# Attention with a sparse feed-forward: the third value product behind the next step's first maxima, the turn of the maxima behind the third maxima

## The reference, cut to what matters

```python
h = layernorm(x)                                  # x: 16 x 512 x 128
q, k, v = (h @ w_lat @ w_heads for each)          # 16 heads of 8
att = softmax(where(causal, q k^T / sqrt(8), -inf))
x = x + layernorm(att v @ w_proj + b_proj)
y = shared_geglu(layernorm(x)) + sum over the top 2 of 12 experts of w_e * geglu_e(layernorm(x))
x = x + layernorm(y)
```

## Time and profile before

| what | value |
|---|---|
| runs | 1266.59, 1270.77, 1272.27 us; median 1270.77 |
| the profiled execution | 1269.61 us, span 1267.8 us |
| mean granted TensorE clock | 0.930 |
| PE busy | 1074.8 us, 85% of the span |
| DVE busy | 837.0 us, 66% |
| ACT busy | 745.3 us, 59% |
| POOL busy | 631.4 us, 50% |

### The profile page before, as it was taken

One profiled execution on the slowest core, in us unless ns is written; L12 is line 12 of the kernel. 1 busy time (PEld: TensorE's weight loads), 2 busy tenths in 40 slices (PEclk: granted clock), 3 DMA queues, 4 the chain that ended last, 5 costly groups with the idle time before them and its releaser, 6 DMA issues.

```text
span 1267.8 us, 31490 instructions
## 1 busy us (share of the span) xinstructions
PE 1074.8 (85%) x8446; PEld 619.5 (49%) x8446; DVE 837.0 (66%) x2411; ACT 745.3 (59%) x1311; POOL 631.4 (50%) x1184
## 2 busy tenths in 40 slices
PE   4789999999999999978888877655899999999765
PEld 2633333333333333323565545322788888888732
DVE  7587777777878777766875556322466666666637
ACT  3777777777767777756544344321566666666616
POOL 4256666666666666644145545554144444444344
PEclk9799999999999999989767887778899999999988
DMA  8223333333333333332611111111222222221156
GB/s 221 69 74 88 96 101 101 91 90 97 95 94 93 96 101 99 91 104 62 223 31 39 37 37 35 37 37 56 51 67 61 62 66 60 62 67 51 47 192 215
DMA packets 135607, 107.47 MB, mean 85 GB/s; under 512 B 32204, under 2 KB 127875, under 8 KB 135539
## 3 DMA queue, kind: packets, MB, share of 16 engines
q1 hardware_dynamic: 124722, 87.45, 24.6%
q0 software_dynamic: 8544, 17.78, 3.9%
q10 hardware_dynamic: 2272, 1.45, 0.4%
HBM read 55.96 MB, written 50.69 MB: 84 GB/s over the span
## 4 chain that ended last, share of the span: by engine, by line
PE 62%; DVE 10%; issue 9%; another core or an unknown queue 7%; ACT 7%; DMA 3%; SPq 1%; ACTq 1%; POOL 0%; DVEq 0%; POOLq 0%
PE ps L1221 11%; PE ps L1386 7%; PE ps L1387 7%; PE ps L1398 7%; DVE maxima L1524 5%; PE ps L1149 5%; PE ps L1180 5%; PE ps L1140 2%; PE ps L1313 2%; PE ps L1332 2%; PE ps L1157 2%; ACT quad_area L973 2%; PE ps L1203 1%; ACT outT_area L918 1%
## 5 line engine op out<-in xcount | busy, mean ns | idle before, releaser
L1524 DVE TENSOR_REDUCE maxima<-ps 128x8 f32<-128x1024 f32 x320 | 387.0, 1222 | 122.6 <-PE ps L1149 109.3
L911 ACT ACTIVATE pT_area<-ps 128x1024 f32<-128x1024 f32 x320 | 327.5, 1025 | 145.1 <-PE ps L1180 144.5
L699 POOL TENSOR_SCALAR_AFFINE_SELECT pT_area<-pT_area 128x256 f32<-128x256 f32 (+1 forms) x448 | 190.4, 439 | 110.9 <-ACT pT_area L911 109.1
L801 POOL DMA_INDIRECT ys_dram<-quad_area,place_cur x139 | 133.1, 957 | 206.3 <-issue 138.2
L791 POOL DMA_INDIRECT xs_dram<-quad_area,idx_cur x128 | 123.3, 963 | 139.5 <-issue 73.0
L1221 PE MATMUL ps<-pT_area,quad_area 128*32 128x512 f32 (+3 forms) x2048 | 190.9, 446 | 0.0
L1180 PE MATMUL ps<-quad_area 64*128 64x512 bf16 (+3 forms) x1024 | 124.9, 301 | 25.5 <-DVE maxima L1524 22.2
L1386 PE MATMUL ps<-quad_area 128*128 128x256 f32 (+1 forms) x456 | 129.8, 367 | 8.1 <-issue 6.8
L1387 PE MATMUL ps<-quad_area 128*128 128x256 f32 (+1 forms) x456 | 128.4, 363 | 0.0
L1149 PE MATMUL ps<-quad_area 61*128 61x128 bf16 (+2 forms) x1792 | 126.8, 244 | 0.0
L1819 DVE SCALAR_TENSOR_TENSOR quad_area<-ps,be_cur,xnT 128x256 f32<-128x256 f32 (+1 forms) x228 | 97.5, 458 | 40.2 <-ACT xnT L1009 37.1
(11 more groups left out here) (237 smaller groups left out, 1665.0 us busy)
## 6 DMA issues: line engine op xcount, KB each, us to landing
qk_dram<-split_area SPq DMA_DIRECT2D x192, 128.0 KB, 2.3
quad_area<-qk_dram SPq DMA_DIRECT2D x256, 96.0 KB, 2.3
row_area<-xs_dram SPq DMA_DIRECT2D x63, 132.0 KB
pT_area<-ys_dram SPq DMA_DIRECT2D x16, 512.0 KB, 5.2
pT_area<-in_L_ffn_We SPq DMA_DIRECT2D x12, 384.0 KB, 7.5
out_dram<-pT_area SPq DMA_DIRECT2D x7, 512.0 KB, 2.9
xs_dram<-row_area SPq DMA_DIRECT2D x5, 528.0 KB, 4.2
split_area<-in_L_ffn_We SPq DMA_DIRECT2D x12, 192.0 KB, 3.8
```

Source lines behind the costliest of these rows:

```text
L699: return pool.affine_select(out=blocks, in_=blocks, compare_op=ALU.is_ge, fill=0.0, base=0, pattern=[[0, count], [1, P]], channel_multipli ...
L801: pool.indirect_dma_start(ys_dram, at, ys[:, ns % 2, h, :], None).then_inc(s_yst[ns % 2], 16)
L911: act.activation(pT[:, gs % 2, n, :], ps[:, bank:bank + 2, :].rearrange("p a b -> p (a b)"), ACT.Exp).then_inc(s_exp, 1)
L1524: dve.tensor_reduce(to, ps[:, bank:bank + 2, :].rearrange("p a (j k) -> p a j k", k=P), AX, ALU.max).then_inc(s_mxf, 1)
```

## The change

The third product is taken from behind "exp" 4 of the step after its quad's and put behind "max" 0 of the step after that, ahead of "exp" 0. The turn of the maxima, behind "exp" 1 so far, goes behind "max" 2, ahead of "exp" 2, in all steps but the first two (g below 0). Nothing is added or removed.

```diff
-PRODUCTS = {("exp", 0): (2, 3), ("exp", 2): (1, 0), ("exp", 3): (1, 1), ("exp", 4): (1, 2)}
+PRODUCTS = {("max", 0): (2, 2), ("exp", 0): (2, 3), ("exp", 2): (1, 0), ("exp", 3): (1, 1)}
...
-                    if (kind, n) == ("exp", 1) and present("max_rows", gs):
+                    if (kind, n) == (("exp", 1) if gs < 0 else ("max", 2)) and present("max_rows", gs):
                         turn_maxima(gs, g)
```

## The result

| | before | after |
|---|---|---|
| median (runs) | 1268.68 us (4) | 1286.7 us (4, from 1280.33 to 1293.76) |
| ratio, first measurement | | 1.0146, 95% interval [1.0092, 1.02] |
| ratio, second measurement | | 1.0116 [1.0071, 1.0161] (6 runs) |
| span of the profiled execution | 1267.8 | 1284.8 |
| mean of the 12 loop turns | 33.67 | 34.50 |

It is slower, as forecast, but by more: 10.1 us were forecast, the attention stage alone took 14.8 us longer, and the first median lay 2.2 us above the range. The mean of the turns is from the first masks of step 6 to those of step 54 (404.09 and 414.01 us), over 12. The second measurement is told at the end of the experiments.

A forecast was written before the change was run, and what follows sets the result against it. PE was taken to pace the attention stage, waiting on DVE's maxima. Terms 7.4 + 0.3 + 0.2 + 2.2 = 10.1 us, added to 1269.61 and 1270.77, gave 1279.7 and 1280.9; forecast 1280.3 us, range 1270.5 to 1284.5.

The forecast's parts named there:

- What bounds the stage, and the turn of the maxima: Attention stage: PE paces it; the turn's wait for ACT is hidden behind DVE, so moving the turn gains 0.
- That rival: Turn's wait for ACT on the path, up to 12.8 us back: 1268.1 (chance 0.05) or 1258.0 us (0.08).
- s1 to s2: Border of second to third step of a four-step loop turn: masks' release stays, +0.57 us each, 13 times, 7.4 us.
- The rival of the wait that moves: First masks at s1 to s2 come earlier with the projection, so the product is covered again: 1270.8 us, chance 0.14.
- s0 to s1: Border of first to second step of a loop turn: masks 0.29 us earlier, net +0.02, 13 times, 0.3 us.
- s2 to s3: Border of third to fourth step of a loop turn: no wait between, no change; possible gain at most 0.2 us a turn.
- s3 to s0: Border of fourth step to next turn's first: product stays ahead of exponential scores' wait for DVE, so nothing changes.
- Sum of PE's work from the fifth exponential scores to the next step's first ones: unchanged: Every step border: the moved product keeps its 0.57 us, only its side of the first masks' wait changes.
- the edge term: Attention stage's end: product loses cover at SP load waits, 1.02 us at the 3.00 wait, 0.57 at two others; 2.2 us.
- the loss behind 1.20 is swallowed by the 1.55 that follows: Attention stage's end: product's loss at the 1.20 us DVE wait vanishes in the next 1.55 us load wait.
- a second low clock: Rival: one of two long waits near the end lowers the clock for 7 us, at most 3.1 us: 1283.4, chance 0.08.
- The forecast's own range: Loss from only the 13 borders (7.4 us) up to the sum with both last-step extras (11.3): 1278 to 1283 us.

The follow-up runs named there:

- second measurement: The changed kernel run again on one chip with the kernel before: ratio 1.0116 [1.0071, 1.0161], loop turn 34.48 us.
- the late normalisation: DVE's normalisation put behind the fifth maxima instead of ahead: in the changed kernel ratio 1.0023, in the kernel before 1.0007.
- the two partial moves: Kernel before with the product moved only at border s1 to s2, ratio 1.0076, or only at the three other borders, ratio 1.0023.
- one item later: Kernel before with the third product moved behind the first exponential scores, ahead of the fourth product, turn of the maxima unmoved: ratio 1.0122 [1.0063, 1.0182].
- the stores behind the loads: SP's blank-row stores moved behind the step's loads and maxima's rows: in the changed kernel ratio 1.0052, in the kernel before 0.9943.
- the combination of three changes: Kernel before with normalisation behind the fifth maxima, blank-row stores behind loads and later turn of the maxima, product unmoved: 1254.26 us, ratio 0.9899.

## Why the prediction was right and wrong

*What bounds the stage, and the turn of the maxima*: right. Only the product moves the loop turn; the turn's wait for ACT is hidden behind DVE, and its own experiment left the loop turn at 33.67. That rival fell.

*s1 to s2*: right in kind and place. The release stayed at 1.61 behind the fifth reduction, the idle time went from 0.39 to 0.96, and the late normalisation shows that DVE's order sets most of it. The rival of the wait that moves fell with it. The size was off: 0.68, not 0.57.

*s0 to s1, s2 to s3, s3 to s0*: 0.02, 0 and 0 forecast, about 0.03, 0.10 and 0 measured.

**The steps that failed are two terms of the sum.**

The first is "Sum of PE's work from the fifth exponential scores to the next step's first ones: unchanged". I moved a product as a block of fixed length. In the new order the same instructions take 0.09 us more, as a product comes 0.32 behind the first maxima's scores and the exponential scores came 0.23 behind them; this is lost at s1 to s2 and at s2 to s3. The measured loop is 9.9 us longer, where mine was 12 x 0.59 = 7.1: 2.8 of the missing 4.7 us of the attention stage (14.8 - 10.1), of which 12 x 2 x 0.09 = 2.2 is this. The 0.32 could not be read before the change, when every product stood behind exponential scores.

The second is the edge term, "2.2 us". The tail holds it and the thirteenth border, so I had 2.8 there. It grew by 4.8 us in the first profile of the change and by 4.9 in the second. The rest of the change's 14.8 us, less than 0.2, is ahead of the loop, where I had 0.2.

Two parts of the term were wrong. That "the loss behind 1.20 is swallowed by the 1.55 that follows" did not hold: the wait of step 58 grew to 1.77 us, and that of step 59 fell only to 1.44, in the second profile to 1.28. And in the tail I had given a second low clock a chance of 0.08 and no place in the sum. It came. In the profile of the changed kernel that was taken again, at the end of the wait for the load of step 61, 2.23 us long, the windows (columns as in the earlier trace rows) show:

```profile
597.00:602.00 5.00, 4.43 (x44) 1.71 (x46) 1.23 (x1) 1.51 (x2) 1.87 (x6) 0.51 0.02 5
602.00:607.00 5.00, 4.76 (x28) 1.61 (x25) 2.36 (x2) 2.20 (x3) 1.18 (x3) 0.50 0.01 2
```

Ten microseconds at the lower of the two levels. The time from step 61 to line 1291 is 31.3 us there, against 27.3 before. In the first profile of the change it came behind step 59's wait of 1.44 us instead:

```profile
580.00:584.00 4.00, 2.56 (x32) 0.83 (x30) 2.38 (x3) 1.45 (x2) 2.35 (x9) 0.81 0.03 6
584.00:588.00 4.00, 3.66 (x36) 1.43 (x33) 2.35 (x2) 3.28 (x5) 1.17 (x3) 0.76 0.76 198
```

Over the whole tail the clock stood at its lower level for 13.7 us in both profiles of the changed kernel and for 6.8 us before. The 6.8 us more cost at most half their length, 3.4 us (an estimate); the term was short by 2.0. The other profiles mostly go the same way: 13.7 us with the product alone moved and with each of the two partial moves, 17.1 one item later, 6.8 with the turn alone. With the stores behind the loads it is 3.4 us for the changed kernel and none for the one before. With the late normalisation, though, it is 6.8 us with the product in either place. That the lost cover brings the low clock on is my reading of this count; no experiment set the clock by itself, and it stays open. Of the clock rival, then, the event came and its chance was too small.

The Trainium skill, "TensorE: Matmul & The Clock Gate", "A second HAM failure mode: psum-queue depth-cycling", has short idles between groups of matmuls throttle the clock again. In the loop of the kernel before and of the changed one this is not borne out: the granted clock is 1.00 in both, with idle waits of 0.96 in every turn of the latter. The two steps at a low clock in the loop of the late normalisation, behind waits of 0.93 and 0.25, speak for it, though the combination of three changes has waits like them in its loop, 0.90 and 0.35, at 1.00 throughout. I had set that rule aside too firmly.

The forecast's own range had a slip as well: 10.1 and both tail terms are 11.2, not 11.3, which ends at 1282, not 1283.

**What the first ratio adds.** Behind the attention stage the time from line 1291 to the first expert matmul was, over all thirteen profiles, 267.1 to 285.5 us. It was 271.6 and 281.5 in two executions of the changed kernel, 267.1 with the turn alone and 284.8 with the late normalisation, with no order by where the product stands. That is more than the change is worth, and of the size by which the whole times of one kernel lie apart (the kernel with the product alone moved: 1272.61 to 1291.26). The median of four runs was 18.0 us above before, 3.2 more than the attention stage lost in the profile; the second ratio, 1.0116, makes 14.7 us of 1270, about what the attention stage lost in both profiles (14.8 and 15.4). The forecast, 10.1 us or a ratio of 1.0080, lies below the interval of the first ratio and inside that of the second, which does not make it right: the terms above stay short. The range erred in leaving only a microsecond for the scatter; three runs of before within 5.7 us had looked like less.

## What to carry to other kernels

Work that stands ahead of a wait is cover for it: before moving it, find what releases the wait and whether that moves along. The same instruction behind the wait cost its full time in one place of four here, 0.67 of 0.83 us a turn; where the product stayed ahead of a wait for DVE's chain (s3 to s0), it cost nothing. And the cure was not on the engine that waits. Large stores behind the loads that are needed next gave 0.6% alone; together with a small operation behind, instead of ahead of, the reduction that frees a buffer, and the later turn of the maxima, 1.0%. The small operation alone gave nothing that the runs could tell.

## What the runs showed of the hardware

- What an instruction follows counts on PE. The fp32 value product starts 0.32 us behind eight bf16 score matmuls of 128 columns, bf16 scores start 0.23 behind the same eight. Two products in a row take 0.79 us, apart 0.57 and 0.36.
- Where the loop jumps back, PE shows 0.46 us of idle "issue" once no value product stands ahead of the masks; with one ahead it did not show. In this loop DVE's later release covered it.
- A wait of 1.44 us was followed by a low clock and one of 2.28 us by none in the same execution, and waits of 1.55 and 1.81 us in another by none. Waits of 0.93 and 0.25 us in one step stood ahead of a granted clock of 0.57 in two turns of twelve: how long a single wait is does not tell alone.
